# A graph network on one core: twenty slots for the walks' own rows, and the edge attributes' copy on ScalarE

## What is computed

```python
x = layernorm(x + sage(x))      # mean of the neighbours, one matrix
x = layernorm(x + gcn2(x))      # two normalised sums over edges, two matrices
x = layernorm(x + gatv2(x))     # 4 heads of 128, edge attributes, then a feed-forward block
x = layernorm(x + gat_gat(x))   # two attention layers of 2 heads of 64
```

```python
xl, xr, e = x @ Wl.T + bl, x @ Wr.T + br, edge_attr @ We.T
z = leaky_relu(xl[src] + xr[dst] + e, 0.2)        # 512 = 4 heads of 128
logit = einsum('ehd,hd->eh', z, att)
```

## Time and profile before

| what | value |
|---|---|
| median of three executions | 5472.02 us |
| profiled execution, and its span | 5479.4 us, 5477.7 us |
| PE, DVE, ACT, POOL busy | 3545.5, 3366.1, 2200.3, 3615.9 us |
| walk e1a, walk e1b | about 966 to 1236 us, 1237 to 1504 us |
| logits of the attention | about 1840 to 2387 us |
| mean granted TensorE clock | 0.842 |

### The profile page before, as it was taken

The page is one execution under the profiler, slowest core; times in us unless marked ns, Lnnn a source line. Parts: engine busy times, 40 slices in busy tenths (PEclk is TensorE's granted clock), DMA queues, the critical chain, the costliest instruction groups (busy, mean ns, idle before and its releaser), DMA issues. The chain is left out here.

```text
span 5477.7 us, 98470 instructions
## 1 busy us (share of the span) xinstructions
PE 3545.5 (65%) x21061; PEld 2458.7 (45%) x21062; DVE 3366.1 (61%) x13936; ACT 2200.3 (40%) x6294; POOL 3615.9 (66%) x4923
## 2 busy tenths in 40 slices
PE   4527699677788498869769999730008995100298
PEld 3427688666666244422256666520007774100133
DVE  6434488444488476678668888641608886253288
ACT  0005477676767233323258888500004441000155
POOL 2747577767645477707668888675765556757698
PEclk9659999999999799989989999855559997555699
DMA  1005498888899622201134444351119895311498
GB/s 29 1 25 160 152 278 262 232 253 239 244 275 284 217 86 52 53 6 38 34 111 140 139 140 143 111 145 37 41 38 293 290 290 168 99 33 41 141 342 300
DMA packets 550994, 816.49 MB, mean 149 GB/s; under 512 B 118566, under 2 KB 267629, under 8 KB 550466
## 3 DMA queue, kind: packets, MB, share of 16 engines
q1 hardware_dynamic: 396820, 559.50, 32.9%
q0 software_dynamic: 69184, 122.90, 9.1%
q10 hardware_dynamic: 84816, 132.30, 6.4%
HBM read 493.48 MB, written 329.46 MB: 150 GB/s over the span
## 5 line engine op out<-in xcount | busy, mean ns | idle before, releaser
L620 POOL DMA_INDIRECT agg_dst<-e_rows,e_put_i x392 | 390.6, 996 | 203.6 <-issue 118.8
L1874 POOL DMA_INDIRECT e_rows<-h,e_other_i x392 | 390.4, 996 | 150.8 <-issue 118.8
L1209 POOL TENSOR_TENSOR n_rstd<-n_rstd,minus_half 128x4 f32<-128x4 f32 x294 | 333.9, 1136 | 23.1
L689 POOL DMA_INDIRECT agg<-e_msg,e_put_i x196 | 195.2, 996 | 192.9 <-DVEq L718 141.6
L1222 ACT ACTIVATE n_o<-n_y_ps,n_shift,n_rstd 128x128 f32<-128x128 f32 x784 | 293.6, 458 | 12.3 <-POOL n_shift L1489 11.8
L364 POOL DMA_INDIRECT by_src<-s_pay_s,s_place_i x196 | 188.4, 961 | 112.6 <-issue 58.8
L1690 POOL DMA_INDIRECT lg_rows<-x,e_other_i x196 | 187.8, 958 | 110.1 <-issue 59.4
L2373 POOL TENSOR_TENSOR n_u<-n_u 128x512 f32<-128x512 f32 x98 | 124.5, 1270 | 206.0 <-DVE n_u L2320 206.0
L895 POOL DMA_INDIRECT x_rows<-x,d_other_i x196 | 186.3, 951 | 111.8 <-issue 58.2
L1714 PE MATMUL lg_z_ps<-gat_wl,lg_tr 128*128 128x512 f32 x392 | 219.1, 641 | 49.2 <-issue 29.9
L1735 ACT ACTIVATE lg_z<-lg_z_ps 128x512 f32<-128x512 f32 x196 | 117.0, 597 | 317.9 <-PE lg_z_ps L1716 308.1
(11 more groups left out here) (510 smaller groups left out, 11730.6 us busy)
## 6 DMA issues: line engine op xcount, KB each, us to landing
n_ag<-agg_dst SPq DMA_DIRECT2D x294, 264.0 KB, 3.9
n_hs<-h SPq DMA_DIRECT2D x196, 264.0 KB, 3.9
n_xs<-x SPq DMA_DIRECT2D x196, 256.0 KB, 4.2
agg_dst<-e_ev SPq DMA_DIRECT2D x196, 132.0 KB
y<-n_o ACTq DMA_DIRECT2D x98, 264.0 KB, 3.5
e1a_fed<-y SPq DMA_DIRECT2D x196, 132.0 KB
m<-e1a_ev SPq DMA_DIRECT2D x196, 132.0 KB
e1b_fed<-m SPq DMA_DIRECT2D x196, 132.0 KB
```

The source lines that it names most:

```text
L620: pool.indirect_dma_start(out=agg, out_offset=bass.IndirectOffsetOnAxis(ap=e.put_i[:, c:c + 1], axis=0), in_=rows[:, c, :], in_offset=None ...
L689: pool.indirect_dma_start(out=agg, out_offset=bass.IndirectOffsetOnAxis(ap=e.put_i[:, c:c + 1], axis=0), in_=msg[:, g % SLOTS, k, 0:out_wi ...
L1209: st(pool.tensor_tensor(rstd, rstd, keep.minus_half[:, :], ALU.pow))
L1874: pool.indirect_dma_start(out=rows[:, c, :], out_offset=None, in_=h, in_offset=bass.IndirectOffsetOnAxis(ap=e.other_i[:, c:c + 1], axis=0))\
```

## The change

`FED` becomes 20, so the ring of own rows in e1a and e1b has twenty slots: twenty loads are issued ahead of each loop, and after the store of tile k SyncE issues the load of tile k+20. All else that reads `FED` follows by itself. In the logits, VectorE's `move` goes; ScalarE makes the copy into `at`, between its two copies of x, and that copy raises `moved`. The copy into `xt_kept` comes after it and raises a new count, `kept`. PE waits before `product` for `moved` alone and before `turn_over` for `moved` and `kept` of two chunks before.

```diff
-EV, FED = 4, 10
+EV, FED = 4, 20
...
-        moved, moved_att = ph.sem("moved"), ph.sem("moved_att")
+        moved, kept = ph.sem("moved"), ph.sem("kept")
...
                     after(pe, moved, turn, c, 2, TURN)
-                    after(pe, moved_att, turn, c, 2, TURN)
+                    after(pe, kept, turn, c, 2, TURN)
...
                     pe.wait_ge(moved, turn * TURN + c + 1)
-                    pe.wait_ge(moved_att, turn * TURN + c + 1)
...
                     act.activation(tr[:, q, :, :], tr_ps[q][:, 0:2, :], ACT.Copy)
 
-                    act.activation(xt[:, bass.ds((turn * TURN + c) * P, P)], tr_ps[q][:, 0, :], ACT.Copy).then_inc(moved, 1)
+                    act.activation(at[:, q, :], at_ps[q][0:PARTS_IN, 0:P], ACT.Copy).then_inc(moved, 1)
+                    act.activation(xt[:, bass.ds((turn * TURN + c) * P, P)], tr_ps[q][:, 0, :], ACT.Copy).then_inc(kept, 1)
...
-                def move(turn, c):
-                    s, k, q = c // GC, c % GC, c % 2
-                    dve.wait_ge(turned[s], turn * GC + k + 1 + turned.base)
-                    after(dve, z_ready, turn, c, 2, TURN)
-                    dve.tensor_copy(at[:, q, :], at_ps[q][0:PARTS_IN, 0:P]).then_inc(moved_att, 1)
...
-                pipeline(dve, (0, split), (4, move), (5, leaky), (6, score), per_turn=TURN, total=J)
+                pipeline(dve, (0, split), (5, leaky), (6, score), per_turn=TURN, total=J)
```

## The result

| | before | after |
|---|---|---|
| median (lowest to highest), four runs each | 5473.11 us (5471.66 to 5479.09) | 5425.9 us (5423.13 to 5428.32) |
| profiled execution, its span | 5479.4, 5477.7 us | 5423.13, 5421.4 us |
| mean granted clock | 0.842 | 0.845 |
| walk e1a, walk e1b, from the first clearing of a bank to the last batch of matmuls | 269.8, 266.2 us | 259.1, 259.2 us |
| logits, PE's first transpose to its last product | 522.7 us | 491.5 us |

The ratio of after to before is 0.9912, with a 95% interval from 0.9899 to 0.9924: 47.2 us less by the medians, where 41 were forecast. The time lies 5 us under the forecast of 5431 and inside its range.

What follows compares the result with a forecast made beforehand. No single engine was taken to bound the kernel: own-row load latency bound the two walks, PE held up by VectorE the logits. -28 and -13 us sum to -41 us, from 5472.0 to 5431 us; range 5418 to 5453.

Steps and rivals of the forecast that it cites:

- The logits, -28 us: Logits: PE stops being the bound, the stage ends eight steps of 2.27 us behind its last gather, 28 us sooner.
- The copy on ScalarE, at 250 ns: Logits: 196 copies moved from VectorE cost ScalarE some 250 ns each, 49 us in all, hidden under PE's pace.
- Slack by z, and the loop's turn holding PE for 2.5 us: Logits: VectorE's leaky maximum has 1.2 us to spare before PE's product; VectorE's loop turn still holds PE some 2.5 us.
- the gathers' 70.6 us: Logits: time in which the gathers of four groups arrive, 4 x 17.65 us, expected to set the pace.
- the 66.1 of the prediction: Logits: PE's expected time for four groups, 28 x 2.27 + 2.5 = 66.1 us, less than their gathers take.
- Twenty slots, -13 us: Walks e1a and e1b: earlier loads end most waits for own rows; six tenths of the possible gain taken, 13 us.
- the ceiling of 21.9: Walks e1a and e1b: most they could give back, 12.7 and 9.2 us, if both follow their gathers as e0 does.
- a share of 0.98: Walks: how full the DMA engines would be at 1.25 us per tile, 0.91 x 1.342 / 1.25.
- three tiles between take and begin: Walks with ten slots: load k+10 is issued after tile k's take and wanted after tile k+3, 4.0 us.
- The walks gain nothing: Rival, walks: four output slots wait for stores to land, so only the logits gain, 5444 us; chance 0.17.
- PE stays the bound: Rival, logits: long gaps return through PE's wait for z, only 14 us gained there, 5445 us; chance 0.12.
- Slower by the clock: Rival, logits: PE pauses for gathers once a group and its clock falls, +58 us, 5530 us; chance 0.03.

Runs made afterwards that it cites:

- e9_half: The changed kernel with only the other end's rows gathered in the logits, 196 gathers in place of 392 (wrong logits): 5390.22 us.
- e8_first: The kernel before, with VectorE's copy of the turned attributes put ahead of its split of the next: 5443.79 us, ratio 0.9949.
- e4_loop: The kernel before, with VectorE's program in the logits written out in place of a loop: 5448.41 us, ratio 0.9966.
- e6_ev2: The changed kernel with two output slots in place of four: 5547.57 us.
- e3_chunk: The changed kernel with a semaphore for each chunk's gathers in the logits in place of one per group: 5412.18 us, ratio 0.9898 to before.
- e5_fed8: The kernel before with eight slots in the ring of own rows in place of ten: 5746.57 us against 5468.37.
- the last set: Four later runs, about a quarter of an hour after the second set, in which the kernel before took 6755.77 us.

## Why the prediction was right, step by step

**The logits, -28 us.** The mechanism held and the size was 3 us short: the stage is 31.2 us shorter in the pair of profiles, and the copy alone gave 32 us. The stage ends with the last gather and not quite eight steps of 2.27 us, as said. The landing took 2.8 us in place of 3.3, and the last product begins 20.4 us behind the last gather's issue, against 21.5 in the sum, which is 1 of the 3 us. Most of the rest is that PE's first transposes and the last gather lie 471.0 us apart and not 472.7.

**The copy on ScalarE, at 250 ns.** It takes 279 ns, near the upper bound of 285, 54.7 us in all, and it is hidden: PE's products wait for no ScalarE any more, and undisturbed its chunks still follow at 2.27 us.

**Slack by z, and the loop's turn holding PE for 2.5 us.** This step came out otherwise. The product's wait for z is 1.0 us in the whole stage, not 2.5 at each turn. I had moved the turn's stall of 2.6 us into the new kernel as it stood; e9_half shows it gone, with its loop kept. The body of VectorE's loop has 28 copies fewer. Why 28 fewer instructions take the whole stall with them, and in e8_first, with the same number as before, 11.2 of 12.9 us remain, no run here settles. The Trainium skill, "Runtime: NRT & Kernel Launch", section "Instruction fetch mechanics", has a taken branch whose target isn't in the engine's two pages of instructions wait for a fetch; that e4_loop, whose VectorE has no branch in the logits, has no stall agrees with that, and the page gives no price. After keeps the branch and has no stall either, so here the branch alone isn't enough. It changed no sum, because PE's four groups come in under the gathers' 70.6 us in any case. That e9_half has 66.2 us for four groups, next to the 66.1 of the prediction, is luck: the stall of 2.5 us that was put in isn't there, and the 28 chunks that were taken at 63.6 us are slower by as much, by the split's 0.5 us a group among others.

**Twenty slots, -13 us.** The waits are gone as expected. In the first pair of profiles the lags fell by 17.9 us of the ceiling of 21.9, and what is left over e0's 9.3 is 2 us a walk; across the four kernels of either kind the traces give 12 us, and by medians the ring alone gave 8.5 (4 to 14 by the interval). So -13 stands within what the runs spread over, but partly by luck: two errors went against each other. I had taken six tenths of the ceiling for fear of full engines, at a share of 0.98. That share scaled all traffic with the tiles, though the gathers ran at their full pace already. Scaled alone, the loads' and stores' 62.9% of before times 161/149 and the gathers' 27.2% make an estimate of 0.95. Measured is 0.93, because the gathers took 25.3% for 161, where they had taken 27.2% for 160. The two queues of before in 1000 to 1200 us:

```profile
q1 hardware_dynamic: 42731, 40.13, 62.9%
q0 software_dynamic: 5096, 10.76, 27.2%
```

Some eight tenths of the ceiling were there in that pair, and the ceiling itself was read from a profile of before whose walks, 270 and 266 us, were the longest of their kind. The ring's three tiles between take and begin were four, which touched no term.

**The rivals.** *The walks gain nothing*: refuted by after itself. A store takes some 2.6 us in e6_ev2 at a share of 0.76; in after, at 0.93, single stores pass the 4.2 us that four slots allow, and their waits sum to 6.8 us in e1a. The Trainium skill, "DMA: Bandwidth & Descriptors", section "Queues, rings and completion order", has each DMA engine consume descriptors in ring order, by which stores stand behind the loads issued before them. With twenty loads ahead of the loop and one ahead of each later store, the waits for stores came to those 6.8 us in a whole walk, so whatever order the rings keep, it has no larger price here. *PE stays the bound*: refuted by the waits before the transposes, by e3_chunk and by e9_half. *Slower by the clock*: PE pauses for the gathers once a group, for 1.5 us on the mean and 2.2 at most, and the granted clock is 1.00 in the window of 1850 to 2310 us. PE's wait in it (us in total, times, longest):

```profile
PE lg_tr_ps L1705 <- DMA lg_rows<-x,e_key_i: 35.5, 24, 2.2
```

## What to carry to other kernels

Count the tiles that go by between the freeing of a ring's slot and the use of what is loaded into it, times the pace, and hold it against a transfer's landing time at the load that the stage will have. Here two slots fewer than ten cost 278 us, and ten more gave back about 12. Before moving work to another engine, look at what stands ahead of it on its own: exchanging two steps gave three quarters of what the move gave. And when a stage ends a fixed number of steps behind its last gather, the next gain is in the signal that lets these steps begin (e3_chunk cut them from 20.4 to 6.6 us), not in the engines between.

## What the runs showed that was not expected

- A loop's turn on VectorE stood for 2.5 to 2.7 us with 28 chunks in its body, and not at all with one copy fewer in each chunk.
- In the last set the same program took 1.24 times as long: engines stood with no releaser known, PE for 229 us of a walk's 494, and for 228 of these before 1540 us, while gathers were issued or shortly behind. PE in e1a there, in order of time:

```profile
1401.96 0.37 PE L937 MATMUL e1a_bank<-y_rows,e1a_hot 128*128 x1 [3.13 <-issue]
1404.77 0.37 PE L937 MATMUL e1a_bank<-y_rows,e1a_hot 128*128 x1 [2.43 <-issue]
1408.97 0.37 PE L937 MATMUL e1a_bank<-y_rows,e1a_hot 128*128 x1 [3.83 <-issue]
1410.38 0.37 PE L937 MATMUL e1a_bank<-y_rows,e1a_hot 128*128 x1 [1.04 <-issue]
```

One matmul every 1.4 to 4.2 us, where after has 24 in 2.94 us in its first profile. It looks as if instructions arrive late as long as gathers are issued, up to some 25 us beyond the last; that is a reading, and no run here tests it. Nor is it shown why the earlier sets, with the same gathers, have nothing of the kind.
- A load of 132 KB landed in 2.5 us in the median with the DMA engines at 0.65 (e5_fed8), in 3.0 at 0.76 (e6_ev2) and in 3.5 at 0.90 (before, up to 4.8): landing time depends on load well before the engines are full.
